# A causal mask inside the exponents' product: 65 further rows in place of a product with the identity

## What is computed

```python
log_fg = log_sigmoid(fgate_preact[..., 0])
cs = cumsum(log_fg, axis=-1)
fg_mat = cs[..., :, None] - cs[..., None, :]
mask = tril(ones((S, S), dtype=bool))
log_D = where(mask, fg_mat + igate_preact[..., 0][..., None, :], -inf)
max_log_D = max(log_D, axis=-1, keepdims=True)
D = exp(log_D - max_log_D)
C = einsum("bhsd,bhtd->bhst", q, k / sqrt(DH)) * D
normalizer = maximum(abs(sum(C, axis=-1, keepdims=True)), exp(-max_log_D))
h = einsum("bhst,bhtd->bhsd", C / (normalizer + EPS), v)
...
x = x + multihead_layernorm(h) * outnorm_weight
x = x + top2_of_8_experts(layernorm(x))
```

## Time and profile before

| | |
|---|---|
| median of 3 runs | 730.92 us (724.64, 730.92, 742.64) |
| profiled execution | 726.55 us |
| its span, first to last instruction | 724.8 us |
| mean granted TensorE clock | 0.893 of 2.4 GHz |
| instructions | 14827 |

### The profile page before, as it was taken

The page is one execution under the profiler, slowest core; times in us unless marked ns, Lnnn a source line. Parts: engine busy times, 40 slices in busy tenths (PEclk is TensorE's granted clock), DMA queues, the critical chain, the costliest instruction groups (busy, mean ns, idle before and its releaser), DMA issues.

```text
span 724.8 us, 14827 instructions
## 1 busy us (share of the span) xinstructions
PE 624.0 (86%) x3464; PEld 484.7 (67%) x3481; DVE 475.6 (66%) x943; ACT 316.1 (44%) x704; POOL 328.0 (45%) x328
## 2 busy tenths in 40 slices
PE   3873699999999999613299999999999999999993
PEld 1331366677677666511178888888888888888883
DVE  3664367677656636889657676776777676676673
ACT  3453445355344324300045555545555555555551
POOL 2223534536336433217535555555555455455542
PEclk9997699799689658655599999999999999999998
DMA  9995554555645632260113333333333333333332
GB/s 272 294 297 173 158 159 152 177 158 164 183 124 160 182 99 87 79 259 0 30 32 60 59 47 57 59 47 56 59 50 53 59 51 52 59 51 52 59 45 23
DMA packets 71530, 76.70 MB, mean 106 GB/s; under 512 B 12686, under 2 KB 63636, under 8 KB 71508
## 3 DMA queue, kind: packets, MB, share of 16 engines
q1 hardware_dynamic: 55508, 50.20, 22.3%
q0 software_dynamic: 15712, 25.73, 19.6%
q10 hardware_dynamic: 288, 0.52, 0.2%
HBM read 53.21 MB, written 23.21 MB: 105 GB/s over the span
## 4 chain that ended last, share of the span: by engine, by line
PE 76%; DVE 8%; issue 5%; DMA 5%; POOL 2%; ACT 2%; SPq 1%; DVEq 0%; ACTq 0%; POOLq 0%
PE bank L1282 10%; PE bank L1284 9%; PE bank L1283 9%; PE bank L1180 9%; PE bank L1194 7%; PE bank L1314 5%; PE bank L1310 5%; PE bank L1311 5%; PE bank L1297 4%; PE bank L1175 3%; DMA qT_scratch<-qt 3%; PE bank L1177 2%; PE bank L1269 2%; PE bank L1243 2%; PE bank L1211 1%
## 5 line engine op out<-in xcount | busy, mean ns | idle before, releaser
L1102 POOL DMA_INDIRECT out_rows<-ys,index x71 | 112.9, 1590 | 155.7 <-DVE ys L987 151.9
L1282 PE MATMUL bank<-w12l,xh 128*128 x284 | 120.8, 425 | 2.2 <-DVE xl L959 2.2
L1284 PE MATMUL bank<-w12h,xh 128*128 x284 | 112.5, 396 | 0.0
L1283 PE MATMUL bank<-w12h,xl 128*128 x284 | 112.5, 396 | 0.0
L993 DVE TENSOR_TENSOR w3l<-w,w3h 128x1024 fp32r<-128x1024 f32 x71 | 87.2, 1228 | 30.8 <-issue 29.9
L1194 PEld LDWEIGHTS bank<-aug,c 128*128 128x128 f32 x512 | 77.1, 216 | 36.5 <-issue 31.4
L788 DVE SCALAR_TENSOR_TENSOR c<-bank,d 128x512 f32<-128x512 f32 x64 | 44.2, 690 | 75.1 <-PE bank L1194 66.8
L662 ACT CAST w3h<-w 128x1024 fp32r x71 | 74.4, 1048 | 20.0 <-issue 20.0
L1093 POOL DMA_INDIRECT xg<-token_table,index x71 | 70.4, 991 | 23.8 <-issue 21.0
L1180 PE MATMUL bank<-qbd,kt 128*128 128x512 f32 x128 | 78.2, 697 | 3.4 <-issue 3.4
L1310 PE MATMUL bank<-w3l,hth 128*128 128x256 f32 x284 | 76.4, 302 | 1.8 <-DVE w3l L993 1.8
(11 more groups left out here) (165 smaller groups left out, 1128.2 us busy)
## 6 DMA issues: line engine op xcount, KB each, us to landing
x<-in_x SPq DMA_DIRECT2D x32, 256.0 KB, 3.0
wst<-in_w12T POOLq DMA_DIRECT2D x26, 256.0 KB, 3.5
aug<-in_ctxv SPq DMA_DIRECT2D x16, 264.0 KB, 3.0
ct<-in_ctxT SPq DMA_DIRECT2D x16, 256.0 KB, 4.6
qT_scratch<-qt SPq DMA_DIRECT2D x16, 256.0 KB, 3.7
kt<-in_ctxT SPq DMA_DIRECT2D x16, 256.0 KB
qbd<-qT_scratch SPq DMA_DIRECT2D x64, 64.0 KB
out_rows<-x SPq DMA_DIRECT2D x16, 256.0 KB, 2.2
```

Source lines behind the costliest of these rows:

```text
L1102: q.indirect_dma_start(out=out, out_offset=bass.IndirectOffsetOnAxis(ap=index[:, j:j + 1], axis=0), in_=YS[o][:], in_offset=None, compute_ ...
L1282: mm(acc, XH[i][:, k, :], wl, start=(k == 0), stop=False)
L1283: mm(acc, XL[i][:, k, :], wh, start=False, stop=False)
L1284: ins = mm(acc, XH[i][:, k, :], wh, start=False, stop=(k == NK - 1))
```

## The change

The mask is no longer a product of its own. LG and RM get 65 further rows (92 in all, MROWS), and the product is made in two halves of 64 queries per head, for each of the four heads: 256 columns each. Row r of the first 64 further ones marks the key r of the half in question in LG; in RM it holds -1e30 at the queries of the half that come before r, and 0 elsewhere. The 65th row is -1e30 in RM throughout; in LG it is 1 for the keys 64 to 127 in the variant for the first half of the queries, and 0 in the other. So LG exists in two variants, and the 24 rows of g are loaded twice per element. For the second half the keys 0 to 63 have no mark and nothing is masked. Both products open and close their part of the bank alone. id_b and mask4 are gone from memory and from the loads.

```diff
-        RM = [sb(f"rm{i}", [PARTS * (NH + 1), NH, S], BF16, on=early) for i in range(2)]
-        LG = [sb(f"lg{i}", [PARTS * (NH + 1), S], BF16, on=early) for i in range(2)]
+        RM = [sb(f"rm{i}", [MROWS, NH, S], BF16, on=early) for i in range(2)]
+        LG = [sb(f"lg{i}", [MROWS, 2, S], BF16, on=early) for i in range(2)]
...
-        LOADS3 = 1 + HG + 2
+        LOADS3 = 1 + HG + 3
...
-                for dst, src in ((ib, ibias), (fb, fbias), (id_b, identb), (mask4, maskT), (io, iota), (numbers, nums)):
+                for dst, src in ((ib, ibias), (fb, fbias), (io, iota), (numbers, nums)):
...
-                    sp.dma_start(LG[i][0:PARTS, :], marks[0:PARTS, 0:S]).then_inc(late_consts, 16)
-                    sp.dma_start(RM[i][PARTS:PARTS * (NH + 1), :, :],
-                                 marks[PARTS:PARTS * (NH + 1), :].rearrange("q (h s) -> q h s", h=NH)
+                    for lo, hi in ((0, PARTS), (GROWS, MROWS)):
+                        sp.dma_start(LG[i][lo:hi, :, :], lgc[lo:hi, :].rearrange("q (a s) -> q a s", a=2)
+                                     ).then_inc(late_consts, 16)
+                    sp.dma_start(RM[i][PARTS:, :, :], rmc[PARTS:, :].rearrange("q (h s) -> q h s", h=NH)
                                  ).then_inc(late_consts, 16)
...
-                    sp.dma_start(LG[i][PARTS:, :], g_dram[b].rearrange("q h s -> (q h) s")).then_inc(in3[i], 16)
+                    for a_ in range(2):
+                        sp.dma_start(LG[i][PARTS:GROWS, a_, :], g_dram[b].rearrange("q h s -> (q h) s")
+                                     ).then_inc(in3[i], 16)
...
-                    mm(bank[n % 2][:], LG[i][:, c * P:(c + 1) * P],
-                       RM[i][:, hg * HG:(hg + 1) * HG, c * P:(c + 1) * P], start=True, stop=False)
-                    mm(bank[n % 2][:], id_b[:], mask4[:], start=False, stop=True).then_inc(e_ready, 1)
+                    for a_ in range(2):
+                        at = c * P + a_ * HALF
+                        ins = mm(bank[n % 2][:].rearrange("p (h q) -> p h q", h=HG)[:, :, a_ * HALF:(a_ + 1) * HALF],
+                                 LG[i][:, a_, c * P:(c + 1) * P],
+                                 RM[i][:, hg * HG:(hg + 1) * HG, at:at + HALF], start=True, stop=True)
+                    ins.then_inc(e_ready, 1)
...
+    key, row = np.arange(S) % P, np.arange(HALF)[:, None]
+    lgc = np.ones((MROWS, 2, S), np.float32)
+    lgc[GROWS:MROWS - 1] = np.stack([key[None] == row, key[None] == row + HALF], axis=1)
+    lgc[MROWS - 1] = np.stack([key >= HALF, np.zeros(S)])
+    rmc = np.full((MROWS, NH, S), MASKED, np.float32)
+    rmc[PARTS:GROWS] = np.tile(np.eye(NH)[:, :, None], (PARTS, 1, S))
+    rmc[GROWS:MROWS - 1] = np.where(row > np.arange(S) % HALF, MASKED, 0.0)[:, None]
```

More of the change, by code:

```diff
@@ L55 @@
 MASKED = -1e30
+HALF = P // 2
+GROWS = PARTS * (NH + 1)
+MROWS = GROWS + HALF + 1
 def wait(eng, sem, value):
@@ L74, in then, with build @@
         self.eng.wait_ge(self.sem, self.base + self.n)
-def build(nc, x, ctx, ctxv, ctxT, gkq, gkk, gkv, ibias, fbias, onw, w12T, w3T, gateT, ident, identb,
-          maskT, trib, marks, iota, nums, floors, spares, out):
+def build(nc, x, ctx, ctxv, ctxT, gkq, gkk, gkv, ibias, fbias, onw, w12T, w3T, gateT, ident, lgc, rmc, trib, iota, nums, floors, spares, out):
     qT_dram = nc.dram_tensor("qT_scratch", (B, P, NG, S), F32).ap()
@@ L105, in build @@
         id_f = sb("id_f", [P, P])
-        id_b = sb("id_b", [P, P], BF16)
         tri = sb("tri", [P, 2, P], BF16)
@@ L121, in build @@
         onwb = sb("onwb", [P, NH, DH], on=early)
-        mask4 = sb("mask4", [P, HG * P], BF16, on=early)
         wst = [sb(f"wst{i}", [P, HID], on=early) for i in range(2)]
@@ L1339 @@
     p, q = np.arange(P)[:, None], np.arange(P)[None, :]
-    marks = np.ones((PARTS * (NH + 1), NH * S), np.float32)
-    marks[PARTS:] = np.tile(np.repeat(np.eye(NH), S, axis=1), (PARTS, 1))
+    key, row = np.arange(S) % P, np.arange(HALF)[:, None]
[5 more added lines that the diff above has]
+    rmc[GROWS:MROWS - 1] = np.where(row > np.arange(S) % HALF, MASKED, 0.0)[:, None]
     ins = {
@@ L1355 @@
         "ident": np.eye(P, dtype=np.float32),
-        "identb": np.eye(P).astype(bf),
-        "maskT": np.tile(np.where(p > q, MASKED, 0.0), (1, HG)).astype(bf),
+        "lgc": lgc.reshape(MROWS, -1).astype(bf),
+        "rmc": rmc.reshape(MROWS, -1).astype(bf),
         "trib": np.concatenate([p < q, np.ones((P, P))], axis=1).astype(bf),
-        "marks": marks.astype(bf),
         "iota": np.broadcast_to(q, (P, P)).astype(np.float32),
```

## The result

| | before | changed |
|---|---|---|
| median (lowest to highest) | 730.73 us (724.64 to 742.64, 4 runs) | 747.19 us (739.35 to 750.37, 4 runs) |
| ratio, 95% interval | | 1.0216 (1.0108 to 1.0323) |
| profiled execution / its span | 726.55 / 724.8 us | 750.37 / 748.6 us |
| mean granted clock | 0.893 | 0.856 |
| first exponents product starts | 79.33 us | 107.37 us |

The times of products are read from TensorE's timeline, the low stretches from the granted clock. Medians are over all executions, while every ratio leaves out executions more than 1.5% above their kernel's fastest. The kernel became slower, by 1 to 3%, and the range to 756 of the forecast of 735 holds that.

A forecast was written before the change was run, and what follows sets the result against it. It took TensorE as the bound at the low clock and a VectorE-GpSimd loop of 12.2 us per element at the high one. From 726.55 us, +1.7 - 1.7 + 8.2 gave about 735 us, range 714 to 756.

The forecast's parts named there:

- constants: Gating stage: about 0.5 MB more of constant loads, not hidden behind its busy DMA engines, adds 1.7 us.
- head: Start of the attention stage: six groups before the first sc get TensorE's gain, 1.7 us less.
- clock: Twelve attention elements, eight high and four low: 178.0 us against 169.8, so 8.2 us more.
- wrong altogether: Sign that the forecast fails: the gating stage or the untouched expert stage moves by more than 3 us.
- TensorE's price: Exponents pair in attention: 512 fewer columns per group save 0.213 us high, 0.427 low; rows in use priced at nothing.
- The loop over sc, GpSimd's chain and the held small product: Second loop in attention, VectorE and GpSimd: stays at 12.2 us per high element, so TensorE waits up to 1.5 us.
- the high elements gain nothing: Attention at the high clock: TensorE's gain turns into waits ahead of L1243; elements stay at 12.2 us.
- In its second or third element: Attention stage: a run at the high clock ends there, not in its fourth element.
- waits alone: Attention stage: clock falls follow TensorE's waits ahead of L1243, now one in nearly every high element and longer.
- Rival 1: Attention stage: the clock keeps its present pattern, falls depend on something other than waits; 721.8 us, chance 0.20.
- Rival 2: Attention stage: L820 slips ahead of GpSimd's block, TensorE's whole gain of 16.0 us arrives; 712.3 us, chance 0.08.
- Rival 3: Attention stage: waits ahead of L1243 keep most elements at 1.2 GHz, eight of twelve low; 766 us, chance 0.22.

The follow-up runs named there:

- e3_before_rows: The kernel before (512 columns, identity product) with LG and RM of 92 rows, the further 65 zero and loaded as 89 rows at once: 739.18 us, ratio 1.016.
- e2_88: The changed kernel with RM's fixed rows loaded as 88 and 1 in place of 89 at once: 717.32 us, ratio 0.986 to the kernel before.
- e7_k65: The kernel before with LG and RM padded from 27 to 65 rows, zeroed on VectorE at the start: 716.86 us, ratio 0.987.
- e8_k64: The kernel before with LG and RM padded from 27 to 64 rows, zeroed on VectorE at the start: 720.50 us, ratio 0.990.
- e4_pool: The kernel of e1_split with GpSimd's weight load issue and split moved ahead of its work on sc: 720.68 us, ratio 0.985 to the kernel before.
- e2_again: The kernel of e2_88 run again unchanged, as a control: 718.66 us, beside 731.53 us for the kernel before.
- e10_k65_gate: The kernel of e7_k65 with the gating product moved behind the next step's first exponents and scores: 706.69 us, beside 731.53 us for the kernel before.
- e1_split: The changed kernel with RM's fixed rows loaded as 24, 64 and 1, LG's as 64 and 1: 720.69 us, ratio 0.991 to the kernel before.

## Why the prediction was right or wrong

*The number held, the main term didn't.* Against the profiled execution the forecast was +1.7 (constants) - 1.7 (head) + 8.2 (clock) = +8.2. Measured were +28.0, -2.7 and -4.1, and +2.5 in the tail and the expert stage: +23.8, before rounding. That 747 lies in the range is luck: the range reached up to 756 for low stretches of the clock, which cost nothing more here, and a term of 1.7 us that was 28 filled it. The prediction had its own sign for this, wrong altogether if the gating stage moved by more than 3 us. It moved by 28.

*Constants: the step that failed.* The prediction priced half a MB at the stage's mean rate, "1.7 us. Lower bound nothing [...]; upper bound 3". The bytes were right. What was wrong is the step from bytes to time, which took the rate of all 16 engines: the 89 rows ran at 27 to 30 GB/s, and the queue stood still behind them. e3_before_rows shows the whole price alone, e2_88 takes 23 us of it away by one row.

*TensorE's price.* Taken was 0.213 us per group at the high clock and 0.427 at the low. Measured, by the medians: 0.32 in the pair and 0.10 ahead of it, 0.42 in all, and at the low level 0.51 (0.93 to 0.43) and 0.12, about 0.63. The prediction's lower bound for the pair (0.24, from the 256-column products of the expert stage) was nearer than its choice. Wrong was the sentence that the rows in use (27 to 92) cost or bring nothing: they bring 0.20 of the 0.42, about half. e7_k65 against e8_k64 shows it, 0.22 against 0.32 us by one row. The earlier trace rows has the sign of it, 0.32 behind the 27-row product and 0.23 behind the 128-row one; the prediction took the 0.107 between them for a load that would stay.

*What arrives.* The loop over sc, GpSimd's chain and the held small product is there: sc to sc 11.86 us, L823 held 0.89 us to the end of the split. The 12.2 us were 0.3 too long. The wait ahead of the gating product came, at 0.68 us instead of up to 1.5. But that "the high elements gain nothing" was wrong. From the gating product at 165.21 us to the next at 175.97, all at the high clock and with the wait of 0.68, are 10.76 us, where 12.2 were charged and 11.56 stood before. In a low element VectorE has time to catch up (the next sc comes after 15.46 us), so the loop held TensorE only at the end of each high run. e4_pool shows that this loop isn't opened by turning GpSimd's order round.

*The clock.* Low stretches of 80 us were forecast, 85.3 came, and e2_again had 85.3. "In its second or third element" was right: high runs now last 13.65 us. But four low elements at 20.1 us and eight at 12.2 was wrong in size: two elements take 27.3 us together, where that count gives 14.8 us per element, 29.7 for two. The stretch got 4.1 us shorter where 8.2 longer was forecast; the high elements at under 12.2 us and TensorE's larger gain per group are what was missing. The cause given, waits alone, is too short: five of e10_k65_gate's seven waits brought no fall.

The rule of the Trainium skill ("TensorE: Matmul & The Clock Gate", section "Why this matters for your kernels") that lays a drop on much longer gaps doesn't describe this kernel: the clock fell after every wait of 0.67 or 0.68 us at the high level in the changed one. The one on SBUF ("SBUF — State Buffer", section "SBUF: two separate sides") has the exclusive hold right, but e4_pool's 2.62 us, over the ends of several GpSimd operations, is more than "for the whole instruction".

*Rivals.* Rival 1 came in time once the constants are mended (e1_split 720.7, forecast 721.8), and e1_split's low stretches sum to the same 61 us. But it isn't its mechanism, as the clock fell at other places and more often (six times to 290 us, before three). Rival 2's price of 16 us wasn't reached by the median of any kernel with halves; at the same clock about 11 of them arrived. Rival 3, slower by the clock alone, didn't come. Slower by over 2% had 0.24. The measured 2.2% (1.1 to 3.2) came from a cause that no rival named.

## What to carry to other kernels

Price a load by how it is spread as well as by its bytes, and read it in the DMA share of its stretch: 0.06 to 0.08 of 16 engines is about one engine. When rows are added to a tile, look at the row count of the load; here 88 and 1 in place of the prime 89 gave back 23 us. When a small product stands between 128-row ones, try it with more than 64 rows before taking columns away from it: here 65 rows, most of them zero, gave the same median as the whole rewriting. And before a gain of 1% is put down to an edit, compare the runs at the same granted clock, and try the edit that should change nothing: 64 rows left TensorE's distances as they were and still came out 1.0% faster.

## What the runs showed that was not expected

- Behind loads of 89 rows of 4 KB a stretch ran at 30 GB/s with all DMA engines together 0.08 busy; as 88 and 1 rows the stretch had 274 GB/s. SyncE's next issue took 12.51 us.
- A bf16 product of 27 or 64 rows next to 128-row products cost about 0.1 us ahead of it and 0.1 us behind it, beside its columns, with 65 or 92 rows next to nothing: 0.32 against 0.22 and 0.21 us behind it, 0.21 against 0.11 ahead.
- The clock varies within one program: 50.9 and 85.3 us low in e2_88 and e2_again. Profiles with 256 columns had 50.9 to 85.3 us, those with 512 columns 22.8 to 61.4, which overlap.
- VectorE's 16-column product was held up to 3.7 us by GpSimd operations in a row.
